# Two attention layers in one kernel: the first layer's fillers, query moves, weight loads, value-weight copies and last two steps reordered

## The chip, the cores and the metric

The kernel runs on one core of a Trainium2 chip. The metric is the device time of one execution in microseconds, the median of several runs. Before the change it is 1479.65 us, the median of 3 runs (1478.13 to 1481.38).

The core has five engines with instruction streams of their own, which wait for one another by semaphores: TensorE (PE, matrix products; the weight loads that precede them are shown apart as PEld), VectorE (DVE), ScalarE (ACT), GpSimd (POOL) and SyncE (SP, which here only issues DMA transfers). ScalarE too can issue transfers.

## What is computed

Two layers follow each other on x (8 batches of 256 queries, 160 channels); both use a context of 8 x 512 x 256 (the second its first rows).

```python
# layer 0: 20 heads of 8 channels; the context is split into 77 text and 435 image rows
q = split_heads(x @ Wq.T)
text, ip = ctx[:, :77], ctx[:, 77:]
o  = softmax(q @ k(text).T / sqrt(8)) @ v(text)        # Wk, Wv
o += softmax(q @ k_ip(ip).T / sqrt(8)) @ v_ip(ip)      # Wk_ip, Wv_ip
x  = merge_heads(o) @ Wo.T + bo + x

# layer 1: 20 heads of 64 channels
n = layer_norm(x, ln1); x = x + attention(n, n,   a1_wq, a1_wk, a1_wv, a1_wo, a1_bo)
n = layer_norm(x, ln2); x = x + attention(n, ctx, a2_wq, a2_wk, a2_wv, a2_wo, a2_bo)
n = layer_norm(x, ln3); h = n @ ff_w1 + ff_b1
x = a * gelu(gate) @ ff_w2 + ff_b2 + x                 # a, gate = halves of h
```

## The kernel before

All products are made in parts: an operand is split into a high and a low part (tiles ending in `hi` and `lo`), and two or three partial products are added up.

**Layer 0.** `narrow_attention_layer` takes the 20 heads of a batch in 5 groups of 4 heads, so there are 8 x 5 = 40 groups, one a step. A step t has four slots s = 0 to 3, and each engine writes its instructions slot by slot in the function `part(t, s)`. In them TensorE makes the scores of group t (`score`), from which VectorE takes the row maxima; it transposes the maxima of group t-1 in slot 1 (`turn_max`; the matmul form `l_pj<-identity,l_negmax`); it makes the turned scores of group t-2 (`turned_scores`), of which ScalarE takes the exponentials; and the weighted sums of group t-3 (`weighted_sums`), whose result ScalarE copies out into `l_sums`. `T_LAG` (2) and `V_LAG` (3) are these distances. In free slots stand the projections of later batches (`q`, `ip`, `text` and `rest` for queries and keys, `v0` to `v3` for values, `out0` and `out1` for the output of an earlier batch) by the table `PLAN`, and `EARLY` and `LAST_PLAN` instead of it at the start and the end. Where no projection stands, `fill` and `fill_early` (table `FILLED`: slot, number, whose bank) put *fillers*: matmuls on old operands whose result nobody reads.

The denominators of a group's softmax come out of the weighted sums as extra rows. SP moves them to `l_den` (`move_dens`), VectorE takes their reciprocals for a whole batch at once, SP spreads these over the partitions with five transfers (`spread_recips` into `l_rb`), and GpSimd multiplies the sums by them (`l_ot`), in the place from which the output projection reads. Before the sums of a later batch's first group may be copied into the same buffer, that multiply must be done.

Keys and queries of a group are stacked on the partitions by transfers from their projections (`stack_keys`, `stack_queries`), and then rounded by GpSimd (`round_stack`); ScalarE rounds the very first group. All of these transfers are SP's: at the start in `begin()`, later in `step(t)`, in the order in which the code stands: inputs of batch b+2 and spreads of batch b-2 in a batch's first step, the denominators of group t-3, and in its third step all stacks of the next batch. SP takes its list in order, and a wait in it holds up all behind it.

**The end of layer 0.** The last batch has no batch after it to hide its chain of denominators, reciprocals, spreads, multiply and output. So its groups are finished in two parts: the first four by one reciprocal and one multiply (`invert_last(0)`, `multiply_last(0)`, `output_last`), the fifth by itself. This lies among the first steps of layer 1, and VectorE does the work, between the row maxima of layer 1's first scores (`a_negmax`).

**Layer 1.** Self attention (a1), cross attention (a2) and the feed-forward part follow. The weights of a1 are loaded and split while layer 0 still runs: SP loads the query and key weights after step `OPEN` (24) and the rest from `OPEN + 7` on. ScalarE copies the high parts of the value weights in six pieces in the slots listed in `WV_HI`, where step 0 of layer 1's own count lies 16 steps ahead of its start, and GpSimd makes the low parts. In the cross attention GpSimd adds up probabilities of several key rows (`sum_keys`, three additions of tile `a_key_sum` a step), and takes the reciprocal square roots of the next layer norm (`pool_rstd`); TensorE reads the key sums after a last addition by VectorE.

## Time and profile before

| what | before |
| --- | --- |
| median of 3 runs | 1479.65 us (1478.13 to 1481.38) |
| profiled execution, its own time | 1479.6 us |
| its span | 1477.8 us |
| TensorE's mean granted clock | 0.991 of full speed |
| TensorE busy | 1448.8 us (98%) |
| VectorE busy | 1065.7 us (72%) |
| ScalarE busy | 784.7 us (53%) |
| GpSimd busy | 463.3 us (31%) |

The span runs from the first to the last instruction of the profiled execution; its own time is the device's. A row of the timeline gives the start, the duration, the engine, the line of the kernel and the operation as out<-in with the number of instructions gathered in the row; in brackets stands the idle time of the engine just before it, and what ended that. The granted clock (PEclk) is the share of full speed that TensorE was given. Layer 0 takes about the first 330 us.

### The profile page before, as it was taken

Reading aid. Unit: us, or ns where it says so; the run is one execution under the profiler, and the core shown is the slowest. Engines: PE = TensorE matmul, PEld = TensorE weight load, DVE = VectorE, ACT = ScalarE, POOL = GpSimd, SP = SyncE. Lnnn points to the kernel's source line nnn. Section 1 sums busy time; section 2 is a strip of 40 time slices with the busy share of each in tenths; the row PEclk is TensorE's granted clock in tenths of the full one; section 3 lists DMA queues with packets and bytes.
Section 4 is the critical chain, followed back from the end, with each engine's and each line's share of the span. In section 5 each row is a group of like instructions: output and inputs, shape, how many; then the busy total and the mean of one; then the engine's idle time right before and its main releaser. Section 6 shows DMA issues by size and latency. Waiting matters only on the chain.

```text
span 1477.8 us, 40867 instructions
## 1 busy us (share of the span) xinstructions
PE 1448.8 (98%) x17914; PEld 1149.7 (78%) x17914; DVE 1065.7 (72%) x1511; ACT 784.7 (53%) x1079; POOL 463.3 (31%) x406
## 2 busy tenths in 40 slices
PE   9999999998999999999999999999999999999999
PEld 7556656567888888888787888888788888878899
DVE  7788887846777777776677676776767677686776
ACT  4777777853564456654354444544444454443444
POOL 3455457531232223433122222222222222222210
PEclk9999999998999999999999999999999999999999
DMA  4433344211000200001010100101010030000000
GB/s 136 128 84 85 83 134 121 47 30 31 2 2 2 100 2 6 2 15 46 24 30 2 30 1 2 30 1 31 2 30 2 2 77 2 2 2 2 2 14 23
DMA packets 32508, 50.43 MB, mean 34 GB/s; under 512 B 7697, under 2 KB 20945, under 8 KB 31953
## 3 DMA queue, kind: packets, MB, share of 16 engines
q1 hardware_dynamic: 32336, 47.88, 11.7%
q8 instruction: 140, 2.29, 0.7%
q14 instruction: 32, 0.25, 0.1%
HBM read 29.18 MB, written 1.31 MB: 21 GB/s over the span
## 4 chain that ended last, share of the span: by engine, by line
PE 85%; DVE 5%; ACT 5%; POOL 3%; issue 2%; DMA 1%; SPq 0%; ACTq 0%; POOLq 0%; DVEq 0%
PE a_pj L1047 8%; PE a_pj L1035 6%; PE l_px L1745 5%; PE a_pj L541 5%; PE a_pv L1069 4%; PE l_pst L1649 4%; PE a_px L1069 4%; PE a_px L584 3%; PE a_px L1090 3%; PE a_pscore L968 3%; PE a_pj L550 3%; PE ff_ph L2249 3%; PE a_px L570 2%; ACT l_probs L1862 2%; PE a_pst L989 2%; PE a_pv L570 2%
## 5 line engine op out<-in xcount | busy, mean ns | idle before, releaser
L1334 POOL TENSOR_TENSOR a_key_sum<-a_probs 128x512 f32<-128x512 f32 x120 | 162.9, 1362 | 443.3 <-ACT a_probs L1155 443.3
L1237 DVE TENSOR_REDUCE a_negmax<-a_pscore 128x2 f32<-128x1024 f32 x160 | 195.6, 1222 | 82.7 <-PE a_pscore L968 82.4
L1155 ACT ACTIVATE a_probs<-a_pst 128x1024 f32<-128x1024 f32 x160 | 164.2, 1026 | 140.2 <-PE a_pst L995 140.2
L2012 DVE TENSOR_REDUCE l_negmax<-l_pscore 128x2 f32<-128x154 f32 x320 | 199.9, 685 | 41.5 <-PE l_pscore L1634 41.0
L1862 ACT ACTIVATE l_probs<-l_pst 128x1024 f32<-128x1024 f32 x160 | 164.0, 1025 | 56.7 <-PE l_pst L1649 54.9
L768 POOL TENSOR_TENSOR a_key_sum<-a_probs 128x1024 f32<-128x1024 f32 x40 | 96.9, 2423 | 219.5 <-ACT a_probs L632 219.5
L708 DVE TENSOR_REDUCE a_negmax<-a_pscore 128x4 f32<-128x1024 f32 x80 | 97.6, 1220 | 40.5 <-PE a_pscore L499 40.5
L1047 PE MATMUL a_pj<-a_wv_hi,a_ct 128*128 128x256 f32 x640 | 111.9, 287 | 1.0
L632 ACT ACTIVATE a_probs<-a_pst 128x1024 f32<-128x1024 f32 x80 | 82.0, 1024 | 38.0 <-PE a_pst L525 38.0
L720 DVE RECIPROCAL a_recip<-a_pv 128x256 f32<-128x256 f32 x40 | 70.3, 1757 | 42.9 <-PE a_pv L575 42.8
L1262 DVE RECIPROCAL a_recip<-a_pv 128x256 f32<-128x256 f32 x40 | 70.2, 1756 | 42.9 <-PE a_pv L1078 42.9
L1035 PE MATMUL a_pj<-a_ct,a_wk_hi 64*128 64x512 f32 x640 | 93.4, 391 | 1.0 <-DVE a_ql L1225 0.9
L1144 ACT ACTIVATE a_neg_t<-a_pscore 128x256 fp32r<-128x256 f32 x40 | 15.4, 385 | 145.5 <-PE a_pscore L1100 145.5
L1047 PEld LDWEIGHTS a_pj<-a_wv_hi,a_ct 128*128 128x128 f32 x640 | 89.6, 189 | 2.7 <-DVE a_kl L1225 2.6
L1144 ACT ACTIVATE a_v<-a_pj 128x1024 f32<-128x1024 f32 x40 | 41.1, 1027 | 94.1 <-PE a_pj L1047 94.1
L989 PE MATMUL a_pst<-a_qh,a_kh 64*128 64x256 f32 x640 | 90.3, 279 | 0.2
L991 PE MATMUL a_pst<-a_qh,a_kl 64*128 64x256 f32 x640 | 89.8, 277 | 0.0
L995 PE MATMUL a_pst<-a_neg_t,a_sel 64*128 64x256 f32 x640 | 89.5, 277 | 0.0
L993 PE MATMUL a_pst<-a_ql,a_kh 64*128 64x256 f32 x640 | 89.4, 276 | 0.0
L1745 PE MATMUL l_px<-l_probs,l_v 128*32 128x256 f32 x1280 | 88.8, 397 | 0.0
L1649 PE MATMUL l_pst<-l_q,l_k 32*128 32x256 f32 x640 | 80.1, 327 | 8.1 <-ACT l_probs L1862 5.6
L1649 PEld LDWEIGHTS l_pst<-l_q,l_k 32*128 32x128 f32 x640 | 49.4, 186 | 46.2 <-ACT l_probs L1862 32.3
(273 smaller groups left out, 3618.4 us busy)
## 6 DMA issues: line engine op xcount, KB each, us to landing
l_rb<-l_recip SPq DMA_DIRECT2D x40, 128.0 KB
l_ct<-in_ctx_t SPq DMA_DIRECT2D x8, 512.0 KB, 4.1
l_k_stack<-l_k_hi SPq DMA_DIRECT2D x64, 64.0 KB, 2.1
a_ct<-in_ctx_t SPq DMA_DIRECT2D x8, 512.0 KB, 4.7
a_ct<-in_ctx_t SPq DMA_DIRECT2D x16, 256.0 KB, 5.3
l_q_stack<-l_q_hi SPq DMA_DIRECT2D x80, 32.0 KB, 1.9
a_raw_wv<-in_a_wv SPq DMA_DIRECT2D x2, 1280.0 KB, 9.1
l_x<-in_x_t SPq DMA_DIRECT2D x8, 256.0 KB, 3.9
```

Source lines behind the costliest of these rows:

```text
L708: nc.vector.tensor_reduce(to, pscore[:].rearrange("p h (q k) -> p h q k", q=QT), AX.X, ALU.max, negate=True).then_inc(max_done, 1)
L989: mm(pst[:, h, to], kh[OWN[h], kb, i, kt], qh[OWN[h], qb, i, :], start=True, stop=False)
L1035: last = mm(pj[:, t, :], wk[hw][OWN[t], s, u * P:(u + 1) * P], cts[b % 2][OWN[t], hc, s, :], start=k == 0, stop=k == len(C_ROWS) - 1)
L1047: last = mm(pj[:, kt // 2, (kt % 2) * STEP_COLS:(kt % 2 + 1) * STEP_COLS], cts[b % 2][:, hc, 2 * s, kt * P:(kt + 1) * P], wv[hw][:, s, u * ...
L1069: mm((pv, px)[x][t * 32:(t + 1) * 32, 0:SQ], v[:, e % 2, kt, t * D1 + x * 32:t * D1 + (x + 1) * 32], probs[:, t, kt, :], start=kt == 0, st ...
L1155: nc.scalar.activation(probs[:, 2 * i:2 * i + 2, 2 * n:2 * n + 2, :], pst[:].rearrange("p h (k q) -> p h k q", k=2), ACT.Exp, scale=SCALE) ...
L1237: nc.vector.tensor_reduce(to, pscore[:], AX.X, ALU.max, negate=True).then_inc(max_done, 1)
L1334: nc.gpsimd.tensor_tensor(key_sums[n][:, two], probs[:, two, 2 * n, :], probs[:, two, 2 * n + 1, :], ALU.add).then_inc(half_summed, 1)
L1649: last = mm(pst[:, h, i * SQ:(i + 1) * SQ], k4[rows, u, kt * P:(kt + 1) * P], q4[rows, u, :], start=True, stop=True)
L1745: last = mm(px[j * ROWS:(j + 1) * ROWS, 0:SQ], vs[m % 2][:, kt, GROUP * u + j, :], probs[g % 2][:, j, kt, :], start=kt == 0, stop=kt == KT ...
L1862: nc.scalar.activation(probs[g % 2][:, 2 * pair:2 * pair + 2, 2 * n:2 * n + 2, :], pst[:].rearrange("p h (k q) -> p h k q", k=2), ACT.Exp, ...
L2012: last = nc.vector.tensor_reduce(to[:, :, k], pscores[s % 2][:, :, keys], AX.X, ALU.max, negate=True)
```

## The change

Several edits, most of them in layer 0's order.

The first three steps are planned anew: the tables `EARLY` and `FILLED` move the second batch's projections and the fillers, `FIRST_SCORES` puts two of group 0's scores into the first slot, and `FIRST_EXPS` takes its exponentials in slots (1, 2) to (2, 1) instead of (2, 0) to (2, 3). In these steps the score comes after the turned scores, and VectorE places the maxima of the group before ahead of the next maximum. The query moves of groups 0 to 2 of the first batch are issued by ScalarE: group 0's three after its copy of the text keys, the six others after it has rounded group 0. Below is TensorE's order from the first score on, two buffers `l0_pscore` by turns (matmuls of `l0_k4` and `l0_q4` into them are scores; those into `l0_pj` or `l0_px` from `l0_k4` alone are fillers; the others are projections of `l0_ct0` and `l0_ct1`, the first and second batch's context), before:

```order
L1634 MATMUL l0_pscore0<-l0_k4,l0_q4 128x512 x2
L1672 MATMUL l0_px<-l0_wc,l0_ct0 128x160 x6
L1634 MATMUL l0_pscore1<-l0_k4,l0_q4 128x512 x2
L1666 MATMUL l0_pj<-l0_ct1,l0_wc 128x512 x6
L1634 MATMUL l0_pscore0<-l0_k4,l0_q4 128x512 x2
L1672 MATMUL l0_px<-l0_wc,l0_ct1 128x320 x6
L1634 MATMUL l0_pscore1<-l0_k4,l0_q4 128x512 x2
L1768 MATMUL l0_pj<-l0_k4 128x256 x8
L1634 MATMUL l0_pscore0<-l0_k4,l0_q4 128x512 x2
L1666 MATMUL l0_pj<-l0_ct1,l0_wc 128x78 x6
L1634 MATMUL l0_pscore1<-l0_k4,l0_q4 128x512 x2
L1777 MATMUL l0_pj<-identity,l0_negmax 128x128 x2
```

and after:

```order
L1654 MATMUL l0_pscore0<-l0_k4,l0_q4 128x512 x2
L1654 MATMUL l0_pscore1<-l0_k4,l0_q4 128x512 x2
L1692 MATMUL l0_px<-l0_wc,l0_ct0 128x160 x6
L1789 MATMUL l0_pj<-l0_k4 128x256 x8
L1654 MATMUL l0_pscore0<-l0_k4,l0_q4 128x512 x2
L1686 MATMUL l0_pj<-l0_ct1,l0_wc 128x512 x6
L1654 MATMUL l0_pscore1<-l0_k4,l0_q4 128x512 x2
L1692 MATMUL l0_px<-l0_wc,l0_ct1 128x320 x6
L1789 MATMUL l0_pj<-l0_k4 128x256 x4
L1654 MATMUL l0_pscore0<-l0_k4,l0_q4 128x512 x2
L1789 MATMUL l0_px<-l0_k4 128x256 x6
L1654 MATMUL l0_pscore1<-l0_k4,l0_q4 128x512 x2
```

The first slot holds two scores in a row and a projection with eight fillers; the key projection `ip` (128x512) comes one score later, four fillers stand behind the value projection `v0`, and six fillers where the text keys (128x78) stood.

The loads of layer 1's weights stand in two steps, `OPEN - 3` (21) and `OPEN + 2` (26), instead of both in step 24. SP's order around the loads (`l_den` are denominators, `l_rb` spreads, `l_k_stack` and `l_q_stack` stacks, `l_ct` and `l_x` inputs) is before:

```order
L1535 DMA l_q_stack<-l_q_lo 32x256
L1557 DMA l_den<-l_sums 8x256 x2
L466 DMA a_raw_wq<-in_a_wq 128x1280
L467 DMA a_raw_wq_rest<-in_a_wq 128x640
L466 DMA a_raw_wk<-in_a_wk 128x1280
L467 DMA a_raw_wk_rest<-in_a_wk 128x640
L1525 DMA l_ct<-in_ctx_t 128x1024
L1526 DMA l_x<-in_x_t 128x512
L1564 DMA l_rb<-l_recip 128x1x256 x5
L1557 DMA l_den<-l_sums 8x256 x3
L1551 DMA l_k_stack<-l_k_hi 32x512
```

and after, around the first of the two:

```order
L1548 DMA l_ct<-in_ctx_t 128x1024
L1549 DMA l_x<-in_x_t 128x512
L1583 DMA l_rb<-l_recip 128x1x256 x5
L1576 DMA l_den<-l_sums 8x256 x2
L466 DMA a_raw_wq<-in_a_wq 128x1280
L467 DMA a_raw_wq_rest<-in_a_wq 128x640
L1576 DMA l_den<-l_sums 8x256
L1570 DMA l_k_stack<-l_k_hi 32x512
L1570 DMA l_k_stack<-l_k_lo 32x512
```

Both weights stood ahead of a batch's five spreads. Now the query weights stand behind them, between the denominators of two steps, and the key weights at the same place one batch later.

The last batch of layer 0 is finished in 3 + 2 groups (`SOON = 3`) instead of 4 + 1: the first reciprocal takes 24 rows and stands one step of layer 1 earlier, the spreads are three and two, and SP moves the last denominators ahead of the first three spreads. The second reciprocal covers all 40 rows, and stands behind the maximum of its place. VectorE's order there (`l_recip` are the reciprocals, `a_negmax` the row maxima of layer 1's first scores, `xs<-xs,l_pj` the addition of batch 6's output), with the semaphores that each instruction waits for, is before:

```order
L708 TENSOR_REDUCE a_negmax<-a_pscore 128x2x2 [waits a1_score_ready]
L701 TENSOR_TENSOR a_qkl<-a_pj,a_qkh 128x1024 [waits a1_qk_hi]
L2054 RECIPROCAL l_recip<-l_den 32x256 [waits l0_spread_in,l0_den_in1]
L2035 TENSOR_TENSOR xs<-xs,l_pj 128x160 [waits l0_biased,l0_pj_ready]
L2054 RECIPROCAL l_recip<-l_den 8x256 [waits l0_end_den_in]
L708 TENSOR_REDUCE a_negmax<-a_pscore 128x2x2 [waits a1_score_ready]
L2035 TENSOR_TENSOR xs<-xs,l_pj 128x160 [waits l0_biased,l0_pj_ready]
L708 TENSOR_REDUCE a_negmax<-a_pscore 128x2x2 [waits a1_score_ready]
```

and after:

```order
L2084 RECIPROCAL l_recip<-l_den 24x256 [waits l0_spread_in,l0_den_in1]
L708 TENSOR_REDUCE a_negmax<-a_pscore 128x2x2 [waits a1_score_ready,a1_negmax_zeroed]
L708 TENSOR_REDUCE a_negmax<-a_pscore 128x2x2 [waits a1_score_ready]
L701 TENSOR_TENSOR a_qkl<-a_pj,a_qkh 128x1024 [waits a1_qk_hi]
L2065 TENSOR_TENSOR xs<-xs,l_pj 128x160 [waits l0_biased,l0_pj_ready]
L708 TENSOR_REDUCE a_negmax<-a_pscore 128x2x2 [waits a1_score_ready]
L2084 RECIPROCAL l_recip<-l_den 40x256 [waits l0_spread_in,l0_end_den_in]
L2065 TENSOR_TENSOR xs<-xs,l_pj 128x160 [waits l0_biased,l0_pj_ready]
```

The first reciprocal moved ahead of the first maximum, the second behind the maximum that it preceded, and it waits for the first spreads besides the last denominators.

The rest: `fill` puts eight fillers in slot 3 and six in slot 2, where it put four. ScalarE's six copies of the value weights stand in later slots, GpSimd's low parts one step later with the bias ahead of them. In the cross attention GpSimd's first two key sums stand ahead of the reciprocal square root, and the third behind it. In layer 0 GpSimd splits inputs before it rounds stacks in a batch's fourth step.

```diff
-    WV_HI = [(12, 0), (12, 1), (12, 3), (13, 0), (13, 1), (13, 3)]
+    WV_HI = [(12, 3), (13, 0), (13, 1), (13, 3), (14, 1), (14, 3)]
...
-            if k == 12:
+            if k == 13:
                 pool.wait_ge(wv_hi, 2)
                 low(wv, 0).then_inc(wv_done, 1)
-            if k == 13:
+                ln.pool_lo(pool, 0, nts[0])
+            if k == 14:
                 pool.wait_ge(wv_hi, 4)
                 low(wv, 1).then_inc(wv_done, 1)
-                ln.pool_lo(pool, 0, nts[0])
-            if k == 14:
+            if k == 15:
+                pool.wait_ge(*ahead["biased"])
...
         def step(d):
+            if here(d - 2):
+                sum_keys(d - 2, [0])
             if norm_at(d, LN_STATS):
                 ln.pool_rstd(pool, norm_at(d, LN_STATS))
             if here(d - 2):
-                sum_keys(d - 2)
+                sum_keys(d - 2, [1])
...
-    EARLY = {(0, 0): ("v3", 0), (0, 1): ("ip", 1), (0, 2): ("v0", 1), (1, 0): ("text", 1), (1, 2): ("v1", 1),
-             (2, 3): ("q", 1), (3, 2): ("v2", 1), (3, 3): ("rest", 1), (4, 2): ("v3", 1)}
-    FILLED = {(0, 3): (8, ("ip", 1)), (1, 1): (4, ("v0", 1)), (1, 3): (8, ("v1", 1)), (2, 0): (4, ("v1", 1)),
-              (2, 1): (6, ("v1", 1)), (2, 2): (4, ("v1", 1))}
+    EARLY = {(0, 0): ("v3", 0), (0, 2): ("ip", 1), (0, 3): ("v0", 1), (1, 2): ("text", 1), (1, 3): ("v1", 1),
+             (2, 2): ("q", 1), (2, 3): ("v2", 1), (3, 2): ("v3", 1), (3, 3): ("rest", 1)}
+    FILLED = {(0, 0): (8, None), (0, 3): (4, ("ip", 1)), (1, 0): (6, ("v0", 1)), (1, 1): (8, ("v0", 1)),
+              (1, 2): (4, ("v0", 1)), (2, 0): (6, ("v1", 1)), (2, 1): (8, ("v1", 1))}
+    FIRST_EXPS = {(1, 2): (0, 0), (1, 3): (0, 1), (2, 0): (0, 2), (2, 1): (0, 3)}
+    FIRST_SCORES = {(0, 0): (0, 1), (0, 1): (), (0, 2): (2,), (0, 3): (3,)}
...
+    def exp_at(t, s):
+        if t <= T_LAG:
+            return FIRST_EXPS.get((t, s))
+        return (t - T_LAG, s) if here(t - T_LAG) else None
...
+    ACT_MOVED = 3
+    def move_queries(eng, u):
+        main = u < GROUPS - 1
+        rows = slice(u * ROWS, (u + 1) * ROWS) if main else slice(0, ROWS)
+        for r, half in enumerate(Q_ROLES):
+            eng.dma_start(q_stack[r:P:4, u, :], q_n[half][rows, 0 if main else 1].bitcast(FP32)).then_inc(
+                stacked[u], 16)
...
-            for u in range(GROUPS if m < B - 1 else GROUPS - 1):
+            for u in range(GROUPS if m < B - 1 else SOON):
                 spread_group(u).then_inc(spread_in, 16)
...
             for group in range(2):
-                stack_queries(0, group)
                 stack_keys(0, group)
             sp.dma_start(ident, dram["ident"]).then_inc(ident_in, 16)
             for group in range(2, GROUPS):
                 stack_keys(0, group)
-                stack_queries(0, group)
+                if group >= ACT_MOVED:
+                    stack_queries(0, group)
...
-            if t == STEPS0 - 1:
-                spread_recips(B - 1)
             if here(t - V_LAG):
                 move_dens(t - V_LAG)
+            if t == STEPS0 - 2:
+                spread_recips(B - 1)
...
-            for _ in range(4):
+            for _ in range(8 if s == 3 else 6):
                 mm((pj if s == 3 else px)[:, 0:SQ], k[:, 0:P], k[:, 0:SQ], start=True, stop=True)
...
+                if what == "text":
+                    act.wait_ge(zeroed, 2)
+                    act.wait_ge(q_low, 1)
+                    move_queries(nc.scalar, 0)
...
             copy(q4[:, 0, :], q_stack[:, 0, :]).then_inc(first_rounded, 1)
+            for u in range(1, ACT_MOVED):
+                move_queries(nc.scalar, u)
...
-                dve.wait_ge(end_den_in, 16)
-            rows = slice(0, n) if k == 0 else slice(n, n + DENS)
+                dve.wait_ge(end_den_in, 16 * (GROUPS - SOON))
+                dve.wait_ge(spread_in, DENS_IN * B - 16 * (GROUPS - SOON))
+            rows = slice(0, (SOON if k == 0 else GROUPS) * DENS)
             nc.vector.reciprocal(recip[rows, :], den[rows, (B - 1) % 2, :]).then_inc(recip_done, 1)
...
-            if GROUPS <= t + 3 < ALL:
-                round_stack(t + 3)
             if u == 3 and b + 2 < B:
                 split_inputs(b + 2)
                 split_rest(b + 2)
+            if GROUPS <= t + 3 < ALL:
+                round_stack(t + 3)
...
-                if d == OPEN:
-                    own["load_weights"](range(2))
+                if d in (OPEN - 3, OPEN + 2):
+                    own["load_weights"]([(OPEN - 3, OPEN + 2).index(d)])
...
-                    if (d, i) == (2, 0):
+                    if (d, i) == (1, 0):
                         first["invert_last"](0)
...
+                    if (d, i) != (1, 1):
+                        own["part"](d, i)
                     if (d, i) == (2, 0):
                         first["invert_last"](1)
-                    if (d, i) != (1, 1):
-                        own["part"](d, i)
```

## Rows read from the trace of the kernel before

**Rows 1.** The page, section 1: busy time, share, instructions of each engine.

```profile
PE 1448.8 (98%) x17914; PEld 1149.7 (78%) x17914; DVE 1065.7 (72%) x1511; ACT 784.7 (53%) x1079; POOL 463.3 (31%) x406
```

**Rows 2.** Stretches of layer 0: bounds, length, engines' busy time, PEclk, DMA, GB/s.

```profile
45.00:50.00 5.00, 4.39 (x48) 2.80 (x48) 4.28 (x8) 3.94 (x6) 3.18 (x6) 1.00 0.34 90
50.00:55.00 5.00, 5.00 (x50) 2.27 (x52) 2.50 (x5) 2.39 (x3) 4.84 (x6) 0.66 0.29 69
...
75.00:80.00 5.00, 4.40 (x48) 2.85 (x40) 4.29 (x7) 3.62 (x5) 2.53 (x4) 1.00 0.29 72
...
220.00:225.00 5.00, 4.54 (x24) 3.97 (x24) 0.27 (x1) 2.65 (x4) 5.00 (x5) 0.66 0.32 79
...
280.00:285.00 5.00, 4.58 (x40) 2.46 (x42) 3.18 (x7) 3.82 (x6) 0.95 (x2) 0.77 0.37 83
...
340.00:345.00 5.00, 4.10 (x34) 3.58 (x32) 2.17 (x3) 2.52 (x5) 2.35 (x1) 0.50 0.53 161
```

**Rows 3.** Chain of waits, 0 to 50 us: start, duration, what ran.

```profile
17.67 0.83 PE l_px L1672 x6
...
22.44 1.15 PE l_pj L1768 x8
...
35.94 0.39 PE l_pst L1649 x2
```

**Rows 4.** Timeline, SP's first query move.

```profile
15.70 0.59 SPq L1535 DMA_DIRECT2D l_q_stack<-l_q_lo  x1
```

**Rows 5.** Timeline, TensorE, the transposition that ends a group (L1777).

```profile
46.16 0.44 PE L1777 MATMUL l_pj<-identity,l_negmax 128*128 128x128 f32 x2
...
54.51 0.44 PE L1777 MATMUL l_pj<-identity,l_negmax 128*128 128x128 f32 x2
...
181.26 0.44 PE L1777 MATMUL l_pj<-identity,l_negmax 128*128 128x128 f32 x2
...
188.36 0.44 PE L1777 MATMUL l_pj<-identity,l_negmax 128*128 128x128 f32 x2
...
216.64 0.44 PE L1777 MATMUL l_pj<-identity,l_negmax 128*128 128x128 f32 x2
...
228.02 0.44 PE L1777 MATMUL l_pj<-identity,l_negmax 128*128 128x128 f32 x2
```

**Rows 6.** Timeline around the spreads of two batches.

```profile
166.95 6.90 SPq L1564 DMA_DIRECT2D l_rb<-l_recip  x5
...
178.34 3.06 POOL L2169 TENSOR_TENSOR l_ot<-l_rb,l_sums 128x512 f32<-128x512 f32 x2 [3.06 <-DMA l_rb<-l_recip]
...
181.46 0.38 ACT L1822 ACTIVATE l_sums<-l_px 128x256 f32<-128x256 f32 x1
...
205.85 3.30 SPq L1564 DMA_DIRECT2D l_rb<-l_recip  x5
...
216.95 3.03 POOL L2169 TENSOR_TENSOR l_ot<-l_rb,l_sums 128x512 f32<-128x512 f32 x2 [3.89 <-DMA l_rb<-l_recip]
...
220.45 0.90 PE L1672 MATMUL l_px<-l_wc,l_ct 128*128 128x160 f32 x6 [2.71 <-ACT l_sums L1822]
```

**Rows 7.** Timeline, the end of layer 0.

```profile
325.52 5.79 SPq L1564 DMA_DIRECT2D l_rb<-l_recip  x4
...
331.41 1.24 SPq L1557 DMA_DIRECT2D l_den<-l_sums  x1
...
333.15 1.63 PE L1783 MATMUL l_pj<-l_wo,l_ot 128*128 128x160 f32 x10
...
335.53 1.74 DVE L2054 RECIPROCAL l_recip<-l_den 8x256 f32<-8x256 f32 x1 [5.22 <-DMA l_den<-l_sums]
...
338.58 0.80 PE L499 MATMUL a_pscore<-a_qkh 64*128 64x256 f32 x4 [3.81 <-DVE a_negmax L708]
```

**Rows 8.** Waits of TensorE, 780 to 1380 us: sum, count, mean.

```profile
PE a_pv L1078 <- DVE a_key_sum L1248: 3.1, 6, 0.5
```

**Rows 9.** Timeline, GpSimd, 790 to 830 us.

```profile
796.71 4.22 POOL L1334 TENSOR_TENSOR a_key_sum<-a_probs 128x512 f32<-128x512 f32 x3
```

54 lines of the change are left out of this document (29 added, 25 removed).

## The prediction

> **What bounds the kernel now.** I read section 1 of the page first: TensorE is busy for 98% of the span [rows 1]. So time can come back only from its few waits, from stretches at the lower clock, and from matmuls that compute nothing. Next the stretches of 5 us over layer 0, for the granted clock. It is 1.00 nearly everywhere (2.4 GHz) and falls in four places: 0.66 at 50 us, 0.66 at 220 us, 0.77 at 280 us, and around the end of layer 0, down to 0.50 (1.2 GHz) at 340 us [rows 2]. Then the chain, the timeline around each place, and the list of TensorE's waits in the cross attention. All four places lie where this change works.
>
> **The front.** From the second score on, the chain between 17.67 and 35.94 is TensorE's own work in an unbroken row [rows 3]; nothing is waited for there. So matmuls added are paid, and waits taken away give nothing. A filler of eight is 1.15 us, 0.144 us each [rows 3]. Before the first step with paired scores (35.94 in the old trace) the old table puts 8+4+8+4+6+4 = 34 fillers, the new one 8+4+6+8+4+6+8 = 44: ten more, +1.4 us. The new table also has the second batch's v2 ahead of that point, six products like those at 17.67, +0.83 us [rows 3]. Its old place in step 3 takes v3, and the place of v3 in step 4 takes six fillers (0.86 us), so that is not given back. Together +2.3 us.
>
> The moves by ScalarE: SP needs 0.59 us to issue one [rows 4]; I take the same for ScalarE, for which no row exists. Three go out before the first rounding, six after it, 3.6 us in which the copy of v3 waits behind them. TensorE reads its place next for v0 in slot (0,3), some 5 us after the rounding by the same prices, so this is hidden. What it costs if not: at twice the issue time 7.1 us are queued and TensorE waits about 2 us. The keys and queries that arrive sooner are no gain, since no row of the chain waits for them.
>
> Back comes one slow stretch. The group that ends at 54.51 took 54.51 - 46.16 = 8.35 us, an ordinary one 188.36 - 181.26 = 7.10 us [rows 5]: 1.25 us, at the lower clock, after a stretch in which TensorE was busy for 4.39 of 5 us [rows 2]. The new table puts six and eight fillers there in place of v3 and four. I take it as gone. Front: +2.3 - 1.25, say +1.0 us; bounds -1.25 (fillers fit into time that the trace shows as work) and +4.5 (issues twice as long, slow stretch stays).
>
> The Trainium skill, TensorE: Matmul & The Clock Gate, sections "What's actually happening" and "HAM oscillation", ties the lower clock to TensorE standing idle. The trace agrees for 220 us, but before 50 us no gap is long, and 4.40 of 5 us at 75 us is followed by no fall. By that rule fillers between short gaps would buy nothing, which is the third rival.
>
> **Loads off the spreads.** The group that ends at 228.02 took 11.38 us, 4.28 more than the ordinary 7.10 [rows 5]. The spreads of reciprocals are issued from 205.85, GpSimd's multiply starts when they have landed, at 216.95, and TensorE waits 2.71 us for the sums' copy behind it [rows 6]; then the clock falls. The lag from first issue to multiply is 11.1 us here and 178.34 - 166.95 = 11.4 us a batch earlier, without weights [rows 6]: the loads do not lengthen it, they start it later, by four issues, 2.0 us. So without them the multiply (3.0 us) and the copy behind it (0.4 us) end at about 205.85 - 2.0 + 11.4 + 3.0 + 0.4 = 218.7, and TensorE wants them at 220.45 - 2.71 = 217.74: some 1 us late still. A batch earlier the multiply ended at 178.34 + 3.06 = 181.40, and the copy started 0.06 us later [rows 6]. SP itself is as slow as TensorE's step. What helps is the front: SP issues nine moves fewer (5.3 us) and TensorE comes some 1 us later. I count 1 to 2 us of that as lead, less two issues for each load in its new place, and take 3.5 of the 4.28 us. Bounds: 0 (late all the same) and -4.28.
>
> **Value weights and fillers at the end of layer 0.** Six copies, as many as before; two leave the slots of step 36, before the fall at 280 us [rows 2], and two land in step 38. They sit between exponentials, where ScalarE has room. GpSimd makes the low parts later, still 4 us ahead of the first projection of layer 1. The bias now comes before them, so the wait for it is empty. I take the slow stretch as gone, -1.25 us as above. Against it, fillers of four become six (four places) or eight (one) in steps 36 to 39, 12 x 0.144 = 1.7 us, of which I put 1.5 on the path, TensorE being the chain there. In the other filled steps, 5, 8 and 9, TensorE waits for an exponential that hides them. Together +0.3 us; bounds -1.3 and +1.7.
>
> **The end, 3 + 2 groups.** The old order issues four spreads from 325.52 to 331.31, the last denominators only behind them at 331.41; VectorE's second reciprocal waits 5.22 us for them and starts at 335.53, with the first maximum of the next group queued behind it, and TensorE, free at 333.15 + 1.63 = 334.78, waits until 338.58, 3.81 us [rows 7]. The new order has the first reciprocal (three groups) before layer 1's first maximum, three spreads some 5 us earlier and the last denominators with no spread left ahead of them. The second reciprocal, 1.74 us as both old ones [rows 7], comes behind that maximum, which frees the score. So 3.8 us go. Late next would be its end, about 333.5, still before the maximum of the score at 334.8. From 340 to 345 the clock is 0.50 with 4.10 us of matmuls [rows 2]; without the wait they take half, 2.05 us more. Together -5.9 us; bounds -2.0 (the first three spreads, which the second reciprocal must let finish, land late) and -7.5 (the slow stretches on either side go too).
>
> **The cross attention.** TensorE waits for the key sums six times, 0.52 us each, 3.1 us in all [rows 8]. In those steps GpSimd's three key sums run in one piece of 4.22 us behind the reciprocal square root [rows 9]. With the first two ahead of it, which have their probabilities by then, only the third follows, and ends some 2 us sooner: -3.1 us; bounds -3.1 and -1.5. The order of splitting inputs and rounding stacks on GpSimd I cost at nothing: a stack is rounded about two steps before its score.
>
> **Sum.** +1.0 - 3.5 + 0.3 - 5.9 - 3.1 = -11.2 us. The profiled execution took 1479.6 us, 1.8 more than its span of 1477.8, and is within 0.1 us of the median of the runs, 1479.65. That gives 1468.4 us.
>
> **The rivals.**
> First, the fillers are free: matmul ends are modelled, so the unbroken row may hide waits. Then the front gives -1.25 and the end of the layer -1.25: 1468.4 - 2.25 - 1.55 = 1464.6 us. For it: DVE too is nearly without gaps in the front, so some of TensorE's time may be waiting. Against: no idle time is shown.
> Second, the spreads stay late: SP has no lead at batch 5, the loads in the two neighbouring batches cost what they cost together. Then 3.5 us are missing: 1471.9 us. For it: the 0.06 us left in batch 4 [rows 6].
> Third, the clock falls at 50 and 280 us all the same: 1468.4 + 2 x 1.25 = 1470.9 us. This is where the page named above points; for it also that 4.39 and 4.40 of 5 us ended differently [rows 2].
> Fourth, slower: each load holds up the spreads of its own batch, because it is issued while the queue still drains those of the batch before. Batches 4 to 7 then each lose what batch 5 loses now: four times 4.28 less the one of today, +12.8 in place of -3.5, 1484.7 us. It decides from about 3 us of delay on per batch. Against: only two more issues lie there per load, and the old loads delayed by their issues only.
>
> **How the numbers follow.** Forecast 0.54 (1466 to 1471), first rival 0.15, second 0.15, third 0.12, fourth 0.04. 0.2%, 3.0 us, is about what a measurement of this kernel tells from no change. Three rivals stay faster by more; with the tails of several bounds at once: faster 0.88, same 0.07, slower 0.05. The range reaches to the first three rivals and somewhat past: 1463 to 1474.
>
> **What would show it.** The paired scores of step 3 start near 38 instead of 35.94; no lower clock near 50 and 280; the copy of sums near 217 without a wait on GpSimd, or one under 1 us; the last denominators' moves with no spread ahead of them, and no wait of TensorE for the maximum near 338; no wait for key sums in the cross attention. Wrong would be: steps 0 to 2 shorter than before, TensorE waiting for the copy of v3, or waits for the multiply in batches 4, 6 and 7.

## The result and the profile after

| | before | changed |
| --- | --- | --- |
| median | 1478.89 us (4 runs, 1477.29 to 1481.38) | 1463.95 us (4 runs, 1462.47 to 1464.30) |
| span of the profiled execution | 1477.8 us | 1462.3 us |
| mean granted clock | 0.991 | 0.998 |

The ratio is 0.9903, with a 95% interval of 0.9875 to 0.9931: faster by 14.9 us, where 11.2 were forecast. The forecast of 1468.4 us was 4.5 us high; its range of 1463 to 1474 holds the time, near its lower end. Beside the last runs the changed kernel took 1463.95 us again (6 runs) and the kernel before 1477.53 us (13 runs, 1474.54 to 1481.94): 13.6 us.

Section 1 of the page, to set beside [rows 1]: TensorE's busy time fell by 5.5 us, though it does 42 matmuls more. The busy time had stretches at the lower clock in it.

```profile
PE 1443.3 (99%) x17956; PEld 1148.1 (79%) x17956; DVE 1070.5 (73%) x1511; ACT 783.9 (54%) x1079; POOL 461.4 (32%) x406
```

The stretches of 5 us that answer to [rows 2] (columns as there), and the two in which the changed kernel's clock falls:

```profile
45.00:50.00 5.00, 5.00 (x59) 3.02 (x52) 4.50 (x9) 3.90 (x6) 3.68 (x5) 1.00 0.32 80
50.00:55.00 5.00, 4.93 (x62) 2.78 (x60) 3.69 (x6) 3.27 (x5) 4.86 (x7) 1.00 0.26 64
...
220.00:225.00 5.00, 5.00 (x62) 3.09 (x62) 3.66 (x8) 3.24 (x4) 4.84 (x6) 1.00 0.31 80
...
280.00:285.00 5.00, 5.00 (x48) 3.54 (x48) 4.11 (x7) 4.99 (x7) 0.00 (x0) 1.00 0.41 90
...
310.00:315.00 5.00, 4.93 (x50) 2.49 (x50) 1.74 (x1) 2.98 (x4) 2.76 (x4) 0.66 0.17 42
...
320.00:325.00 5.00, 5.00 (x51) 2.89 (x50) 0.00 (x0) 3.52 (x8) 0.00 (x0) 0.66 0.23 54
...
340.00:345.00 5.00, 4.36 (x48) 3.55 (x48) 2.97 (x6) 1.79 (x3) 2.35 (x1) 1.00 0.00 0
```

At 50, 220, 280 and 340 us the clock is at 1.00 now. What is left are two short falls to 0.66, at 310 and 320 us; the old trace had them too, as 0.79 to 0.87 in each of the four stretches from 310 to 330 us.

The transpositions that end groups 3, 4, 27 and 28, TensorE's timeline, to set beside [rows 5]:

```profile
47.15 0.44 PE L1798 MATMUL l_pj<-identity,l_negmax 128*128 128x128 f32 x2
...
53.97 0.44 PE L1798 MATMUL l_pj<-identity,l_negmax 128*128 128x128 f32 x2
...
216.14 0.44 PE L1798 MATMUL l_pj<-identity,l_negmax 128*128 128x128 f32 x2
...
224.35 0.44 PE L1798 MATMUL l_pj<-identity,l_negmax 128*128 128x128 f32 x2
```

Group 3 ends 0.99 us later than before, group 4 takes 6.82 us instead of 8.35, group 28 takes 8.21 instead of 11.38. Around the spreads of that batch (beside [rows 6]: SP's spreads, GpSimd's multiply, ScalarE's copy of the sums, TensorE behind it):

```profile
203.66 7.25 SPq L1583 DMA_DIRECT2D l_rb<-l_recip  x5
...
214.81 3.05 POOL L2201 TENSOR_TENSOR l_ot<-l_rb,l_sums 128x512 f32<-128x512 f32 x2 [4.67 <-DMA l_rb<-l_recip]
...
217.89 0.38 ACT L1846 ACTIVATE l_sums<-l_px 128x256 f32<-128x256 f32 x1 [1.61 <-POOL l_ot L2201]
...
218.33 0.90 PE L1692 MATMUL l_px<-l_wc,l_ct 128*128 128x160 f32 x6 [1.09 <-ACT l_sums L1846]
```

The spreads start 2.2 us earlier, the lag of 11.15 us to the multiply is the old one, GpSimd ends it 1.61 us late for the copy (under 1 us was to be seen), and TensorE waits 1.09 us instead of 2.71. The end of layer 0, beside [rows 7], and below it the two waits of TensorE there that answer to the old one's place (sum, count, longest):

```profile
316.13 3.42 SPq L1583 DMA_DIRECT2D l_rb<-l_recip  x3
...
324.71 0.60 SPq L1576 DMA_DIRECT2D l_den<-l_sums  x1
...
326.36 1.23 DVE L708 TENSOR_REDUCE a_negmax<-a_pscore 128x4 f32<-128x1024 f32 x1
327.50 1.74 DVE L2084 RECIPROCAL l_recip<-l_den 40x256 f32<-40x256 f32 x1
```

```profile
PE l_pst L1669 <- ACT l_probs L1886: 3.1, 3, 1.6
...
PE a_pscore L593 <- DVE a_negmax L708: 0.4, 1, 0.4
```

The wait of 3.81 us for the first maximum is gone: the maximum stands at 326.36, ahead of the second reciprocal. Of the last two groups' denominators only the first group's go ahead of the three spreads, otherwise than the section on the change says; the last group's are moved at 324.71, 5.2 us after the spreads were issued, and nothing is queued ahead of them.

In the cross attention the waits of [rows 8] are gone, and one of 0.2 us each for a maximum has come up seven times (first row; 740 to 1380 us). GpSimd's timeline in the step of [rows 9] shows two key sums, the square root, and the third sum alone:

```profile
PE a_pscore L969 <- DVE a_negmax L1238: 1.2, 7, 0.2
```

```profile
781.90 1.28 POOL L1336 TENSOR_TENSOR a_key_sum<-a_probs 128x512 f32<-128x512 f32 x1 [9.79 <-ACT a_probs L1156]
784.36 1.29 POOL L1336 TENSOR_TENSOR a_key_sum<-a_probs 128x512 f32<-128x512 f32 x1 [1.17 <-ACT a_probs L1156]
785.83 0.70 POOL L293 TENSOR_TENSOR a_ln_rstd<-a_ln_var,a_ln_half 128x2 f32<-128x2 f32 x1 [0.17 <-DVE a_ln_var L289]
786.61 0.19 POOL L295 TENSOR_TENSOR a_ln_shift<-a_ln_minus_mean,a_ln_rstd 128x2 f32<-128x2 f32 x1
786.75 1.29 POOL L1336 TENSOR_TENSOR a_key_sum<-a_probs 128x512 f32<-128x512 f32 x1
```

A table by stage, from the transpositions in TensorE's timeline (two profiled executions of each kernel, the second ones from the runs below; the product of key sums counts from its weight load; us):

| stage | before | changed | forecast |
| --- | --- | --- | --- |
| start to the end of group 4 | 54.51, 53.21 | 53.97, 53.88 | +1.0 |
| groups 5 to 27 | 162.13, 162.12 | 162.17, 162.09 | 0 |
| group 28 (batch 5's multiply) | 11.38, 11.02 | 8.21, 7.32 | -3.5 |
| groups 29 to 35 | 49.78, 49.80 | 49.79, 50.82 | 0 |
| groups 36 to 39 (value weights) | 30.54, 29.21 | 29.70, 29.63 | +0.3 |
| end of layer 0, to layer 1's first product of key sums | 47.66, 46.34 | 41.36, 41.46 | -5.9 |
| to the first transposition of the cross attention | 356.68, 356.76 | 356.86, 356.68 | 0 |
| cross attention, to its last transposition | 682.88, 682.89 | 678.00, 678.04 | -3.1 |
| to the end of the span | 82.24, 82.25 | 82.24, 82.18 | 0 |

From the first pair the sum is -15.5 us, from the second -11.5. A stage that differs between them by more than a few tenths holds something that comes and goes from execution to execution.

### The profile page after: what moved, and what is told of

Read it like the earlier page. It is cut to its first block, busy times and chain, and to the rows that moved or that the text cites. A ratio compares the mean times of both kernels' runs of the same rounds, so it can differ in the third digit from the quotient of the medians.

```text
span 1462.3 us, 40956 instructions
## 1 busy us (share of the span) xinstructions
PE 1443.3 (99%) x17956; PEld 1148.1 (79%) x17956; DVE 1070.5 (73%) x1511; ACT 783.9 (54%) x1079; POOL 461.4 (32%) x406
## 4 chain that ended last, share of the span: by engine, by line
PE 84%; DVE 6%; ACT 4%; SPq 3%; DMA 1%; issue 1%; POOL 0%; ACTq 0%
PE a_pj L1048 8%; PE a_pj L1036 6%; PE a_pj L541 5%; PE l_px L1765 4%; PE a_pv L1070 4%; PE a_px L1070 4%; PE l_pst L1669 3%; PE a_px L584 3%; PE a_pscore L969 3%; PE a_px L1091 3%; PE a_pj L550 3%; PE ff_ph L2281 3%; PE a_px L570 2%; PE a_pst L990 2%; PE a_pv L570 2%; PE a_pst L996 2%
## 5 line engine op out<-in xcount | busy, mean ns | idle before, releaser
L1145 ACT ACTIVATE a_v<-a_pj 128x1024 f32<-128x1024 f32 x40 | 41.1, 1027 | 93.3 <-PE a_pj L1048 93.3
L1070 PE MATMUL a_pv<-a_probs,a_v 128*32 128x256 f32 x1280 | 84.7, 382 | 0.1
```

What stands on the lines that cost most here:

```text
L1070: mm((pv, px)[x][t * 32:(t + 1) * 32, 0:SQ], v[:, e % 2, kt, t * D1 + x * 32:t * D1 + (x + 1) * 32], probs[:, t, kt, :], start=kt == 0, st ...
```

## The experiments

Each kernel is the changed one with one edit, unless it says otherwise, and ran beside the kernel before; the stages above are read from its profile.

**The kernel before, once more** (`r_before_again`; no edit).

> The kernel before, a second profiled execution; nothing is changed. Theory A (its four slow stretches come from its order): lower clock again near 50, 220, 280 and around 310 to 345 us, steps 4 and 36 take 8.2 to 8.7 us, the step of batch 5 11.0 to 11.7 us; 1477 to 1481 us. Theory B (the clock and the landing of the spreads differ from execution to execution, as the end of layer 0 did among the changed kernels: no fall in two of five profiles, two falls in three): at least one of the stretches at 50 and 280 us is missing (its step then takes 6.8 or 7.3 us), or the step of batch 5 differs by more than 0.7 us; 1474 to 1481 us.

Measured: 1475.36 us in its one run. The clock near 50 and 280 us (columns as in [rows 2]), then TensorE's wait in step 4 and the transposition that ends it (the one before starts at 46.39):

```profile
50.00:55.00 5.00, 4.88 (x58) 2.73 (x58) 3.58 (x8) 3.31 (x4) 4.84 (x6) 1.00 0.29 75
...
280.00:285.00 5.00, 4.92 (x54) 2.86 (x54) 3.46 (x7) 5.00 (x8) 0.00 (x0) 1.00 0.37 89
```

```profile
50.10 0.39 PE L1649 MATMUL l_pst<-l_q,l_k 32*128 32x256 f32 x2 [0.54 <-ACT l_probs L1862]
...
53.21 0.44 PE L1777 MATMUL l_pj<-identity,l_negmax 128*128 128x128 f32 x2
```

Theory B for these two places. The same instructions with the same wait of 0.54 us took 6.82 us, at full clock, where the first profile had 8.35. Group 36 took 7.26 instead of 8.59. So the slow stretches at 50 and 280 us do not come with every execution of the old order, and their loss in the changed kernel's first profile is no sure gain of the change. How often they come can't be told from two profiles; none of the twelve with the new order of the front, the changed kernel's and its variants', has a lower clock at 50 us. At 220 us and at the end the fall came again (group 28 took 11.02 us, the end 46.34).

**Loads together again** (`e1_loads_together`).

```diff
-                if d in (OPEN - 3, OPEN + 2):
-                    own["load_weights"]([(OPEN - 3, OPEN + 2).index(d)])
+                if d == OPEN:
+                    own["load_weights"](range(2))
```

> The changed kernel (1463.95 us) with the query and key weights of layer 1 loaded together in step 24, as before. Theory A (the place of the loads alone is what batch 5 gains: its multiply ran 0.5 us relative to TensorE no earlier in batches 2 to 4, though SP issues nine moves fewer): the step of batch 5 that took 11.38 us before and 8.21 us after takes 11.0 to 11.6 us again, TensorE waits some 2.7 us for the sums' copy, the clock falls there; 1466.8 to 1467.4 us. Theory B (the prediction's: half of the gain is SP's lead from the moves that ScalarE issues): the step takes 9.3 to 10.2 us; 1465.0 to 1466.0 us.

**Query moves by SP again** (`e2_moves_by_sp`).

```diff
             for group in range(2):
+                stack_queries(0, group)
                 stack_keys(0, group)
...
-                if group >= ACT_MOVED:
-                    stack_queries(0, group)
+                stack_queries(0, group)
...
-                    move_queries(nc.scalar, 0)
...
-            for u in range(1, ACT_MOVED):
-                move_queries(nc.scalar, u)
```

> The changed kernel with all query moves of the first batch issued by SP again, in SP's old order. Theory A (SP waits for data in the first batches, its lead is not built there): the multiply of batch 5 ends when it ended, its step stays within 0.2 us of 8.21; what changes is the front alone: the first stacks are rounded later, and TensorE, which has no idle time in the row there, is late by 0 to 1.5 us in steps 0 to 2; 1464 to 1465.5 us. Theory B (the lead comes from the moves): the multiply of batch 5 is 1 to 2 us later against TensorE, its step takes 9.2 to 10.2 us; 1465 to 1467 us.

Measured: 1464.75 us (1462.31 to 1468.13) with the loads together, 1464.35 us (1463.26 to 1465.69) with the moves by SP; both not to be told from 1463.95. Group 28 took 8.18 us with the loads together, as in the changed kernel, and 7.09 with the moves by SP. Loads together, SP's spreads, the multiply, and TensorE's wait:

```profile
204.85 5.88 SPq L1583 DMA_DIRECT2D l_rb<-l_recip  x5
...
215.24 3.05 POOL L2201 TENSOR_TENSOR l_ot<-l_rb,l_sums 128x512 f32<-128x512 f32 x2 [3.59 <-DMA l_rb<-l_recip]
...
218.76 0.90 PE L1692 MATMUL l_px<-l_wc,l_ct 128*128 128x160 f32 x6 [1.07 <-ACT l_sums L1846]
```

The first spread goes out 1.2 us later than at 203.66, but the five are issued in 5.88 us instead of 7.25, and the multiply starts 1.35 us ahead of the transposition at 216.59, as it did in the changed kernel (214.81 against 216.14). Both theories fail in part: neither the loads' place nor the moves, taken back alone, brings the old step of 11 us back. Both taken back together were not tried. With the moves by SP the first three groups end within 0.02 us of the changed kernel's (25.16, 32.38, 40.03), so in the front they bring nothing either. In that profile group 38 took 10.28 us, behind a wait of 0.69 us for the sums' copy and at a clock of 0.66 (290 to 295 us).

**Four fillers again** (`e3_fill_four`).

```diff
-            for _ in range(8 if s == 3 else 6):
+            for _ in range(4):
```

> The changed kernel with four fillers everywhere in the free slots, as before, instead of six and eight; the table of the first three steps stays. Theory A (the fillers hold the clock): the lower clock comes back in step 4 (near 50 us) and in step 36 (near 280 us), each of these steps is 1.2 to 1.5 us longer (6.82 becomes 8.0 to 8.4, 7.27 becomes 8.3 to 8.6), other filled steps are at most 0.4 us shorter; 1465.5 to 1466.8 us. Theory B (fillers are paid and the clock stays up because of the earlier exponentials at the front and the value weights' later copies at 280 us): steps 36 to 39 are 1.0 to 1.7 us shorter in all, nothing comes back; 1462.0 to 1463.2 us.

Measured: 1464.91 us (1463.82 to 1465.65). Step 4, TensorE's wait and the clock:

```profile
51.23 0.39 PE L1669 MATMUL l_pst<-l_q,l_k 32*128 32x256 f32 x2 [0.54 <-ACT l_probs L1886]
```

```profile
50.00:55.00 5.00, 4.46 (x58) 2.55 (x58) 3.82 (x7) 3.46 (x4) 4.86 (x6) 1.00 0.27 68
```

Neither theory's time came. With four fillers the wait for the exponential is back, 0.54 us, the step takes 6.82 us all the same, the clock stays at 1.00; group 36 takes 7.26 us and group 37 0.10 less. So the additional fillers cost nothing there: they fill a wait. In this execution the clock did not need them; one profile can't show that it never does, but the runs' mean granted clock, 0.997 to 0.998, is that of the changed kernel. (Group 38 took 8.89 us, 0.91 of it a wait for the sums' copy behind a multiply, the same lag of the spreads as in batch 5.)

**Key sums in one piece again** (`e4_keys_whole`).

```diff
-            if here(d - 2):
-                sum_keys(d - 2, [0])
             if norm_at(d, LN_STATS):
                 ln.pool_rstd(pool, norm_at(d, LN_STATS))
             if here(d - 2):
-                sum_keys(d - 2, [1])
+                sum_keys(d - 2)
```

> The changed kernel with GpSimd's three key sums of the cross attention in one piece again, behind the reciprocal square root. Theory A (the split gives what the six steps of the trace lost, 0.70 us each and 0.07 us in the step behind, more than the 0.52 us that the row of waits shows): 4.3 to 4.9 us slower, 1468.2 to 1468.9 us, each of six steps 17.03 instead of 16.33 us. Theory B (the split gives the 3.1 us of the row, the rest of the 4.9 us that the cross attention became shorter has another cause): 1466.8 to 1467.3 us, and the steps come back only to 16.85 us.

Measured: 1468.82 us (1466.83 to 1471.5), 4.87 above the changed kernel, and the cross attention takes 682.94 us, 4.94 more. Theory A. TensorE at the end of such a step, first with the sums whole, then in the changed kernel:

```profile
789.47 0.60 PE L1079 MATMUL a_pv<-a_key_sum,a_ones 128*32 128x256 f32 x4
790.58 0.62 PE L1079 MATMUL a_pv<-a_key_sum,a_ones 128*32 128x256 f32 x4 [0.50 <-DVE a_key_sum L1249]
791.13 0.44 PE L1101 MATMUL a_pscore<-identity,a_negmax 128*128 128x128 f32 x2
```

```profile
791.77 0.61 PE L1079 MATMUL a_pv<-a_key_sum,a_ones 128*32 128x256 f32 x8
792.32 0.44 PE L1101 MATMUL a_pscore<-identity,a_negmax 128*128 128x128 f32 x2
```

The eight products took 1.66 us from start to transposition in two pieces, and 0.55 in one, 1.11 less. The wait of 0.5 us in the row is only the time after the modelled end of the first four, which stand there with 0.60 us, about as long as all eight together (0.61). Some of the 1.11 comes back elsewhere in the step, partly as the new waits for a maximum: the step is 0.70 us shorter (16.33 against 17.03), six times, and the step behind it by 0.04 to 0.45.

**The old end** (`e5_end_four_one`): `SOON = 4`, SP's spreads and both reciprocals in their old places.

```diff
-    SOON = 3
+    SOON = 4
...
-            if t == STEPS0 - 2:
+            if t == STEPS0 - 1:
                 spread_recips(B - 1)
+            if here(t - V_LAG):
+                move_dens(t - V_LAG)
...
-                    if (d, i) == (1, 0):
+                    if (d, i) == (2, 0):
                         first["invert_last"](0)
```

> The changed kernel with the end of layer 0 as before: 4 + 1 groups, SP's and VectorE's old order there. The stretch from the transposition of group 39 to layer 1's first product of key sums took 47.66 us before, and 41.4 us (two slow stretches) or 38.9 us (none) in profiles of the changed end. Theory A (the queue order costs a wait of 3.8 us and this wait brings the fall to the lowest clock behind it): 46.5 to 48 us again, 1469 to 1471.5 us. Theory B (the 3.8 us are the whole of it, the falls there come and go by themselves): 42.7 to 45.3 us, 1466 to 1468.5 us.

**The second reciprocal ahead of the maximum** (`e6_recip_first`).

```diff
+                    if (d, i) == (2, 0):
+                        first["invert_last"](1)
                     if (d, i) != (1, 1):
                         own["part"](d, i)
-                    if (d, i) == (2, 0):
-                        first["invert_last"](1)
```

> The changed kernel with one difference: VectorE's second reciprocal of the last batch ahead of the row maximum again instead of behind it; the groups stay 3 + 2. Theory A (the order on VectorE decides: the maximum queues behind a reciprocal that waits for the last denominators, which land near 327.4, and TensorE's next score behind the maximum): the maximum starts near 329.2 instead of 326.4, TensorE waits 0.5 to 3 us for it; 1464.5 to 1468 us. Theory B (the grouping and SP's order decide, since the last denominators land 4 us after their issue with no spread ahead of them in either order): no wait for the maximum over 0.5 us; 1462.5 to 1464.3 us.

Measured: 1468.48 us (1466.8 to 1474.0) with the old end, 4.5 above the changed kernel; the end takes 46.6 us, with a wait of 3.3 us for the maximum and a clock of 0.52 behind it. Theory A by the stretch; the time lies at the top of B's range, just under A's. With the reciprocal first: 1465.98 us (1462.81 to 1479.71), end 41.1 us. VectorE and SP there:

```profile
340.53 0.60 SPq L1576 DMA_DIRECT2D l_den<-l_sums  x1
...
342.29 1.75 DVE L2084 RECIPROCAL l_recip<-l_den 40x256 f32<-40x256 f32 x1 [0.33 <-DMA l_den<-l_sums]
...
343.96 1.16 DVE L708 TENSOR_REDUCE a_negmax<-a_pscore 128x4 f32<-128x1024 f32 x1
```

Theory B by the mechanism, though the median lies in A's range: the last denominators are there 1.76 us after their issue, the reciprocal waits 0.33 us, and TensorE's next score has no wait for the maximum in the list. With the old end they landed 3.9 us after their issue at 325.65, behind four spreads, and the reciprocal waited 4.72. So the gain doesn't come from the place of the second reciprocal on VectorE; what differs is what stands ahead of the denominators on the queue. The grouping and the earlier first reciprocal, which start the spreads earlier, were not tried apart from that. (The profiled execution of this kernel is the longest of its runs, for a reason that lies ahead of the edit; it stands in the last section.)

**Value weights copied at the old place** (`e8_value_weights_early`).

```diff
-    WV_HI = [(12, 3), (13, 0), (13, 1), (13, 3), (14, 1), (14, 3)]
+    WV_HI = [(12, 0), (12, 1), (12, 3), (13, 0), (13, 1), (13, 3)]
```

> The changed kernel with ScalarE's copies of the value weights in the old slots, two steps earlier, and GpSimd's low parts with them. Theory A (two copies in step 36 delay an exponential and start the fall near 280 us): step 36 takes 8.3 to 8.7 us instead of 7.27, lower clock near 280; 1464.8 to 1466 us. Theory B (the fall at 280 us comes and goes by itself): step 36 takes 7.2 to 7.4 us, the steps 37 to 39 differ by less than 0.5 us; 1463 to 1464.3 us.

Measured: 1468.75 us (10 runs, 1462.25 to 1477.68). Group 36 took 7.48 us and the clock at 280 us was 1.00: theory B by the step. The time is worse than A's, but in the profile it lies elsewhere: group 28 took 12.26 us, more than 50 us ahead of the first copy that the edit moves, with a wait of 2.39 us and the clock at 0.50 behind it.

```profile
219.75 1.57 PE L1691 MATMUL l_px<-l_wc,l_ct 128*128 128x160 f32 x6 [2.39 <-ACT l_sums L1845]
```

```profile
220.00:225.00 5.00, 5.00 (x24) 4.30 (x24) 0.00 (x0) 1.96 (x3) 4.92 (x6) 0.50 0.32 83
```

The runs say more than the profile: seven of the ten are above 1467.41 us, the highest of the changed kernel's ten, and their mean granted clocks are 0.987 to 0.998 against 0.997 to 0.999, though the lowest run is below the changed kernel's lowest. So the old place seems to cost some 5 us, through the clock; where and how is not shown.

**The changed kernel once more** (`r_after_again`; no edit).

> The changed kernel again, nothing changed, beside the kernels below. Theory A (the step of batch 5 and the slow stretches differ from execution to execution, as the second profile of the kernel before and the kernels that leave these places alone showed): single runs from 1462 to 1470 us, the median 1463.5 to 1466 us; the step of batch 5 takes 7.1 to 12.3 us in the profile and need not be 8.21. Theory B (the order fixes them, the differences in the experiments came from their edits): runs within 3 us of 1463.95, the step 8.1 to 8.3 us, lower clock at 310 and 320 us only.

Measured: 1463.95 us again (1462.81 to 1467.41); group 28 took 7.32 us, and group 33 7.88 with a wait of 0.77 us for batch 6's multiply. Theory A. Both falls at the end came again.

**No fillers in the front** (`e7_front_no_fillers`).

```diff
-    FILLED = {(0, 0): (8, None), (0, 3): (4, ("ip", 1)), (1, 0): (6, ("v0", 1)), (1, 1): (8, ("v0", 1)),
-              (1, 2): (4, ("v0", 1)), (2, 0): (6, ("v1", 1)), (2, 1): (8, ("v1", 1))}
+    FILLED = {}
```

> The changed kernel without any filler in layer 0's first three steps (44 matmuls less that compute nothing). Theory A (fillers there are paid, TensorE being the chain): at 0.12 us each steps 0 to 2 are 4 to 5.3 us shorter (the transposition of group 2 at 35 to 36 instead of 40.03), and no wait takes their place; 1459 to 1461 us if the clock holds. Theory B (they stand where TensorE would wait for row maxima, stacks or exponentials): steps 0 to 2 are shorter by under 1.5 us in all, waits of 3 us or more appear there and the clock falls in the first 40 us; 1463 to 1467 us.

Measured: 1470.11 us (1468.33 to 1473.43), 6.2 us slower. TensorE's three longest new waits in the front (sum, count, longest; 0 to 60 us), and the clock:

```profile
PE l_pst L1668 <- DVE l_q L2048: 1.0, 1, 1.0
PE l_pst L1668 <- ACT l_probs L1885: 0.7, 1, 0.7
PE l_pscore L1653 <- DVE l_negmax L2041: 0.6, 1, 0.6
```

```profile
30.00:35.00 5.00, 4.30 (x20) 2.60 (x17) 3.23 (x7) 2.05 (x2) 2.19 (x3) 0.50 0.77 211
35.00:40.00 5.00, 5.00 (x32) 3.30 (x35) 2.93 (x5) 2.44 (x4) 1.27 (x1) 0.50 0.91 293
```

Group 0 ends 1.5 us earlier, then TensorE waits for a rounded query, an exponential and a maximum, and the clock is at 0.50 from 30 to 40 us: group 2 ends at 43.51 instead of 40.03. Theory B in direction, and dearer than it said: the three steps are 3.5 us longer, not shorter. Here fillers do hold the clock; the mean granted clock of all six runs is 0.990 to 0.992, where the changed kernel's are 0.997 to 0.999. The profiled execution, the shortest of the six, is 4.2 us longer in span than the changed kernel's first: 3.5 in the front and 2.0 in group 28 (10.22 us), against 1.4 less from group 36 to the end of layer 0.

**SP relieved** (`e10_sp_relieved`), and **fillers at the end besides** (`e11_relieved_fillers`).

```diff
+    ACT_SLOTS = [(3, 2), (3, 3), (4, 2)]
...
                     stack_keys(b + 1, group)
-                    stack_queries(b + 1, group)
+                    if group < GROUPS - 1:
+                        stack_queries(b + 1, group)
...
+            if b + 1 < B and (u, s) in ACT_SLOTS:
+                if (u, s) == ACT_SLOTS[0]:
+                    act.wait_ge(q_low, b + 2)
+                    wait_rounded(act, GROUPS * b + GROUPS - 1)
+                move_queries(nc.scalar, GROUPS - 1, [ACT_SLOTS.index((u, s))])
...
-            elif s >= 2 and V_LAG <= t < ALL:
+            elif s >= 2 and V_LAG <= t < ALL or (t, s) in ((ALL, 2), (ALL + 1, 2)):
                 fill(t, s)
```

(The last two lines are the second kernel's alone; `move_queries` takes the one role to move.)

> The changed kernel with the three query moves of the last group of each later batch issued by ScalarE (one each in slots (3, 2), (3, 3) and (4, 2)) instead of SP: 1.8 us a batch less for SP. Theory A (SP's list is full from batch 2 to batch 5, its batch takes 36 to 37 us against TensorE's 35.4, and the lag that gathers is what TensorE waits for in batch 5): the spreads of batch 5 are issued 3 us or more earlier against TensorE, its step takes 7.1 us in the profile, and single runs lie closer together; 1461.5 to 1463.5 us. Theory B (the landing of the spreads, 11 us after the first issue, decides, and ScalarE's moves delay exponentials): the step stays above 7.5 us or the steps with the moves grow by 0.2 us or more each; 1464 to 1468 us.

> The kernel with SP relieved as in the run before, and six fillers each behind the turned scores of slot 2 in the first two steps behind layer 0's last score, where TensorE waits 1.6 and 1.4 us for an exponential. Theory A (the gap there lets the clock fall at 310 and 320 us, which costs 2.5 us: 41.4 against 38.9 us from the transposition of group 39 to the first product of key sums): no lower clock from 305 to 330 us, the stretch takes 38.7 to 39.2 us; 0.5 to 2.5 us below the kernel with SP relieved alone. Theory B (the clock falls there or not whatever the fillers do, as fillers of four or of eight made no difference at 50 us): the stretch takes 41 to 42 us, or the same time in both kernels within 0.5 us.

Measured: 1463.38 us (1460.93 to 1464.05) and 1461.47 us (1460.42 to 1461.95). SP relieved, the spreads of batch 5 and GpSimd's multiply:

```profile
199.19 6.66 SPq L1586 DMA_DIRECT2D l_rb<-l_recip  x5
...
211.65 3.07 POOL L2211 TENSOR_TENSOR l_ot<-l_rb,l_sums 128x512 f32<-128x512 f32 x2 [0.65 <-DMA l_rb<-l_recip]
```

The spreads go out 17.8 us ahead of the transposition at 216.98 that ends group 27, against 12.5 us in the changed kernel and 10.8 before; the multiply starts 5.3 us ahead of it, in the second kernel 6.0, more than in any profile without the edit (at most 3.98). Group 28 takes 7.09 us (7.41 in the second kernel, without a wait for the sums). So a full SP is the lag that TensorE waited for: between the spreads of batches 4 and 5 it needed 36.9 us in the changed kernel and 35.6 here, where five steps of TensorE take 35.4. It is paid for in two steps: group 3 takes 0.41 us more and group 15 0.28, where ScalarE's moves delay exponentials. Theory A by mechanism; its gain of 0.6 us is within the noise of single runs.

With the fillers at the end, the clock where it fell before, and TensorE's row with the wait that the fillers shorten:

```profile
310.00:315.00 5.00, 4.83 (x75) 3.32 (x72) 2.59 (x2) 2.62 (x4) 3.00 (x4) 1.00 0.12 28
...
320.00:325.00 5.00, 5.00 (x73) 4.11 (x64) 1.97 (x3) 2.81 (x7) 0.00 (x0) 1.00 0.20 44
```

```profile
306.24 0.98 PE L1784 MATMUL l_px<-l_k 128*128 128x256 f32 x6
307.91 0.50 PE L1673 MATMUL l_pst<-l_q,l_k 32*128 32x256 f32 x4 [0.70 <-ACT l_probs L1890]
```

The wait is 0.70 us instead of 1.6, no lower clock is left anywhere in layer 0, and the end takes 38.84 us: theory A, 1.9 us below the kernel without these fillers. The mean granted clock is 1.000 in all five runs, in one of six without the fillers. The ratio to before is 0.9888 (0.9870 to 0.9906); this version beats both kernels, all its runs lying below the lowest of the changed kernel.

## Why the prediction came out as it did

The time lies in the range, but outside the 1466 to 1471 us to which the forecast itself gave 0.54, and nearest to the first rival. The second pair's sum of -11.5 us is near the -11.2 partly by luck: 1.75 us more came back in the cross attention, and 1.0 each was missing at the end and in groups 29 to 35, where TensorE waited for batch 6's multiply.

**The front, +1.0 us: the sum was near, its terms were not.** By group 3 the cost was 0.99 us in the first pair and 0.68 in the second (47.07 against 46.39), where +2.3 was forecast. What failed is "matmuls added are paid, and waits taken away give nothing": the chain called the row unbroken, but fillers there stand in time that would be waiting, as the front without them shows. The -1.25 us for the slow stretch was counted as sure, but the old order had it in one execution of two; and it was sized against another step of the batch: without the fall this step takes 6.82 us, so the fall cost 1.53. Against an execution without it the front costs 0.7 us, and the paired scores of step 3 start at 36.88, not near 38. ScalarE's six moves took 4.3 us (15.81 to 20.10), where 3.6 were forecast, the copy of v3 waited behind them for 3.44 us, and TensorE did not wait, as forecast.

**Loads off the spreads, -3.5 us: right in size, wrong in cause.** Group 28 lost 3.2 and 3.7 us. Taken back alone, the loads' place changes nothing that stands out of the noise (8.18 us), and neither do the moves taken from SP. In eight profiles of kernels with the new fillers in the front and the new place of the loads, this step took 7.09 to 12.26 us, and in the two of before 11.38 and 11.02. What decides is how far SP's list, which is full from batch 2 on, has fallen behind by then: in the eight the multiply starts 0.01 to 3.98 us ahead of the transposition of group 27, 2.1 on average, and before it started 0.31 behind and 0.03 ahead of it. That lead sets the wait: in all nine profiles in which TensorE waits there, the wait and the lead add up to 2.40 to 2.45 us (1.09 and 1.33 in the changed kernel, 2.71 and -0.31 before). Of what group 28 lost, 1.6 and 2.2 us are wait; the other 1.5 are the lower clock, which does not follow the wait's length. Relieving SP takes the wait away. The lead can run out later as well, which the prediction named as a sign of being wrong: TensorE waited 0.77 us for batch 6's multiply in one profile of the changed kernel, and group 38, batch 7's, took 7.9 us in both, where it took 7.56 before. Which edit gave the changed kernel that lead of 2 us on average is not settled; GpSimd's new order of splitting and rounding, counted at nothing, was not tried alone.

**Value weights and fillers, +0.3 us: within it by the second pair.** +0.4 us there; -0.8 in the first, where the old trace's fall at 280 us had come by chance. The fillers' term was wrong: twelve more cost nothing where 1.5 us were put on the path. The stretch, -1.25 us, was counted as sure and stands in one execution of two; whether the later copies gain something elsewhere, as the ten runs with the early ones suggest, is open.

**The end, -5.9 us: right.** -6.3 and -4.9 us; the old end in the changed kernel takes 46.6 us, 5.2 more. The mechanism is the one named (the denominators behind four spreads, 3.8 us of wait, the half clock behind it). The second reciprocal's place on VectorE, which the working leant on, plays no part. Not counted were the falls at 310 and 320 us, which the change left: 2.5 us, which two of ten profiles of this end do not show (38.9 us there, with the loads together and with the key sums whole, and with the same longest wait of 1.6 us), and which two sets of six fillers take away.

**The cross attention, -3.1 us: the step that was mis-sized.** It measured -4.9, shown by the split alone. The price was read as the idle time in the row of waits, 0.52 us, but the step lost 0.70 and its successor some more: the idle time starts at a modelled end, 0.60 us behind the start of four products, though all eight take no longer than that when nothing is missing.

**The rivals.** The first, fillers free, gave 1464.6 us, nearly the time measured, and its mechanism is the one shown by the fillers taken back to four: they stand in waits. Its 3.8 us are not the whole of the difference, though: 1.8 come from the cross attention, and what it gave for slow stretches came in one pair of two. The second, spreads late all the same, holds in single executions (12.26 us). The third pointed the right way, in that a short gap near 50 and 280 us does not decide the clock, though the falls that it expected there did not come in the changed kernel's two profiles. The granted clock was 0.66 behind such a wait of 0.55 us in one execution of the old order and 1.00 behind one of 0.54 in the next; it fell to 0.50 in the front without fillers, and stood at 1.00 at the end of layer 0 once the wait of 1.6 us was filled to 0.70. The Trainium skill, TensorE: Matmul & The Clock Gate, section "HAM oscillation — how this bites in real kernels", holds idle time of TensorE responsible for the fall. By that rule the trace agrees in direction at 220 us, where the old order waited 2.71 and 2.37 us and the clock was 0.66 behind both; at 50 us the same idle time bears it out in one execution and not in the other. Nor does the length of the wait sort the falls at 220 us: behind 0.54 us the clock fell to 0.71 with the key sums whole, and behind 1.09 it stayed at 1.00 in the changed kernel. What decides there is open. The fourth rival did not come.

The Trainium skill, DMA: Bandwidth & Descriptors, section "Issuing engines are not separate DMA queues", says that issuing from several engines saves the issuing engine's own time alone. The trace agrees: from the first spread's issue to the multiply it is 12.5 us with SP relieved and 11.15 without, so nothing landed faster; what moved was the issue.

## What to carry to other kernels

Take a second profile of the kernel before, ahead of any forecast: a slow stretch that is there in one execution of two is no sure gain for any order. Price a wait by the step that it lengthens, not by the idle time in its row, where the engine's ends are modelled; and price a filler by what its slot would otherwise wait for. An issuing engine whose list is full falls behind batch by batch, and its lateness shows where the slack has run out, not where it is made.

## What had not been expected

The clock can stay down at 0.50 for a long stretch of full work: in one execution it did from 275 to 310 us with TensorE busy for all 5 us of each 5, after a last wait of 0.19 us; that run took 1479.71 us where the same kernel's other four took 1462.81 to 1466.34. And executions of one and the same program differ within one session, by 4.6 us for the changed kernel (1462.81 to 1467.41) and by up to 17 for the kernel before (1473.21 to 1490.41, 17 runs beside the old end); in the profiles the differences lie in when the spreads land and in the clock.
